# One group for the 64-column matmuls of a window pair in a shifted-window attention layer

## The reference

```python
# x: (16, 56, 56, 384) f32; 12 heads of 32; windows of 7x7 = 49 tokens; image shifted by 3
x + attention(group_norm(x, 32 groups))
# attention(x):
x = roll(x, (-3, -3)); q, k, v = split(x @ w_qkv.T)              # per window and head
dots = q @ k.T * 32 ** -0.5 + pos_emb[relative] + mask           # 49 x 49
out = softmax(dots) @ v
out = roll(out @ w_out.T + b_out, (3, 3))
```

## Time and profile before

| | |
|---|---|
| median of 3 runs | 4584.31 us |
| profiled execution | 4584.81 us, of which its span is 4583.0 us |
| mean granted TensorE clock | 0.998 |
| busy share | PE 96%, PEld 65%, DVE 88%, ACT 50%, POOL 50% |
| the chain that ended last | PE 74%, DVE 16%, issue 7%, ACT 2% |

### The profile page before, as it was taken

One profiled execution on the slowest core, in us unless ns is written; L12 is line 12 of the kernel. 1 busy time (PEld: TensorE's weight loads), 2 busy tenths in 40 slices (PEclk: granted clock), 3 DMA queues, 4 the chain that ended last, 5 costly groups with the idle time before them and its releaser, 6 DMA issues.

```text
span 4583.0 us, 164167 instructions
## 1 busy us (share of the span) xinstructions
PE 4390.2 (96%) x64360; PEld 2981.1 (65%) x64360; DVE 4046.9 (88%) x9283; ACT 2275.8 (50%) x4225; POOL 2282.0 (50%) x1933
## 2 busy tenths in 40 slices
PE   3999999999999999999999999999999999999998
PEld 1666666666666666666666666666666666666665
DVE  5898898989989998898989989899898988999886
ACT  0555555455554545555555455555555555555554
POOL 1455445455554554555455455545545545554454
PEclk9999999999999999999999999999999999999999
DMA  4344344334343433443343443334434433434332
GB/s 122 103 106 107 99 107 116 94 108 114 99 109 105 108 104 103 107 109 98 105 119 95 108 112 100 107 106 108 105 97 109 115 95 107 115 98 108 98 95 60
DMA packets 231099, 478.93 MB, mean 105 GB/s; under 512 B 39009, under 2 KB 140898, under 8 KB 222818
## 3 DMA queue, kind: packets, MB, share of 16 engines
q1 hardware_dynamic: 230338, 468.43, 38.6%
HBM read 159.99 MB, written 77.07 MB: 52 GB/s over the span
## 4 chain that ended last, share of the span: by engine, by line
PE 74%; DVE 16%; issue 7%; ACT 2%; SPq 0%; DMA 0%; POOL 0%; DVEq 0%; POOLq 0%; ACTq 0%
PE ps_pj L1087 24%; PE ps_pj L1083 13%; PE ps_post L1181 13%; PE ps_post L1172 5%; PE ps_sa L1121 4%; PE ps_st L1121 3%; PE ps_pv L1165 2%; DVE mt L928 2%; PE ps_st L1150 2%; PE ps_pv L1164 2%; PE ps_pv L1163 2%; DVE atl L907 2%; DVE mw L917 2%; PE ps_pj L1071 2%; DVE st L701 1%
## 5 line engine op out<-in xcount | busy, mean ns | idle before, releaser
L554 POOL TENSOR_TENSOR pl<-pf,ph 64x588 f16<-64x588 f32 x512 | 732.1, 1430 | 1622.3 <-ACT ph L669 1595.0
L599 ACT ACTIVATE qk<-ps_pj 128x392 f16<-128x392 f32 x768 | 381.9, 497 | 978.7 <-PE ps_pj L1087 978.7
L669 ACT ACTIVATE ph<-ps_st,sc 64x588 f16<-64x588 f32 x1024 | 772.5, 754 | 6.5
L1087 PE MATMUL ps_pj<-xh,wh 128*128 128x392 f16 x2304 | 765.2, 332 | 5.5 <-POOL xl L529 4.6
L1087 PE MATMUL ps_pj<-xh,wl 128*128 128x392 f16 x2304 | 764.6, 332 | 0.0
L1087 PE MATMUL ps_pj<-xl,wh 128*128 128x392 f16 x2304 | 764.5, 332 | 0.0
L575 POOL TENSOR_TENSOR rb<-tq,cst 128x588 bf16<-128x588 bf16 x512 | 701.2, 1370 | 48.1 <-ACT tq L658 8.1
L529 POOL TENSOR_TENSOR xl<-xn,xh 128x392 f16<-128x392 f32 x384 | 343.4, 909 | 599.0 <-DVE vl L860 293.0
L865 DVE TENSOR_TENSOR qk<-ps_pj,qk 128x392 f16<-128x392 f32 x768 | 432.8, 564 | 228.3 <-ACT qk L599 225.4
L664 ACT ACTIVATE pf<-ps_st,sc 128x588 f32<-128x588 f32 x512 | 384.7, 751 | 359.1 <-PE ps_st L1121 359.1
L953 DVE TENSOR_TENSOR pl<-pf,ph 64x588 f16<-64x588 f32 x512 | 543.4, 1061 | 0.5 <-ACT ph L669 0.5
(11 more groups left out here) (107 smaller groups left out, 9582.0 us busy)
## 6 DMA issues: line engine op xcount, KB each, us to landing
stack<-qk SPq DMA_DIRECT2D x1536, 147.0 KB
sx<-in_x SPq DMA_DIRECT2D x66, 1176.0 KB, 7.0
xs<-in_x SPq DMA_DIRECT2D x384, 84.0 KB
out<-xb SPq DMA_DIRECT2D x384, 84.0 KB
xs<-in_x SPq DMA_DIRECT2D x384, 63.0 KB
out<-xb SPq DMA_DIRECT2D x384, 63.0 KB
xs<-in_x SPq DMA_DIRECT2D x128, 66.0 KB
out<-xb SPq DMA_DIRECT2D x128, 66.0 KB
```

Source lines behind the costliest of these rows:

```text
L554: nc.gpsimd.tensor_tensor(pl[PAD:, :, PAD:PAD + N], pf[PAD:, :, :], ph[PAD:, :, PAD:PAD + N], ALU.subtract).then_inc(s_pl[1], 1)
L669: e = nc.scalar.activation(ph[rows, :, w * PAD:w * PAD + N].rearrange("p (a h) n -> p a h n", a=2), ps_st[rows, :, 0:HH * N].rearrange("p ...
L1087: m = mm(ps_pj[bank][:, 0:RT].rearrange("p (w n) -> p w n", w=NW), wa[:, c, o:o + 128], xa[:, b, c, :, 0:N], **on)
```

## The change

`transposed_scores` writes its bias with four matmuls of 64 output partitions instead of two of 128, and all of a pair's bias matmuls come before its 24 score matmuls. On PE, `transposed_scores(t - 1)` moves to the start of step k, directly ahead of `scores(t)`, and `shift_rows(t)` moves up from behind `project_out` to directly behind `attend`. The other engines' orders are changed to match: ACT takes `pf` first and `tq` before `ph` and `xh`; DVE makes the maxima before `atl` and the first slot's units; POOL makes `rb(t)` before `pl(t - 1)`, and the residual last.

```diff
 # POOL, step()
                     if not (tk.last and k >= 4):
                         x_lows(tk, k)
-                    if not (tk.last and k + 3 >= 8):
-                        residual(t + 3, n, k + 3)
-                    if not (tk.first and k < 1):
-                        split_probabilities(t - 1, ...)
-                        pool.wait_ge(s_pl[1], t)
-
                     pool.wait_ge(s_tc, t + 1)
+                    need(pool, s_st, t)
                     nc.gpsimd.tensor_tensor(
                         rb[:, :, :, :], ...
                         ALU.mult).then_inc(s_rb, 1)
+                    if not (tk.first and k < 1):
+                        split_probabilities(t - 1, t + 1)
+                        pool.wait_ge(s_pl[1], t)
+                    if not (tk.last and k + 3 >= 8):
+                        residual(t + 3, n, k + 3)
 # ACT, step()
+                    if not (tk.first and k < 1):
+                        probabilities(t - 1)
                     if not (tk.first and k < 3):
                         attended_high(t - 3)
                     if not (tk.last and k >= 4):
                         units(tk, k, 0)
+                    shift_rows(t)
+                    if not (tk.first and k < 1):
+                        probabilities_high(t - 1)
+                    if not (tk.last and k >= 4):
                         x_highs(tk, k)
                         units(tk, k, 1)
-                    if not (tk.first and k < 1):
-                        probabilities(t - 1)
-                    shift_rows(t)
-                    if not (tk.last and k >= 4):
                         units(tk, k, 2)
 # DVE, step()
                     logits(t, tk, k)
                     maxima(t, k)
-                    if not (tk.last and k >= 4):
-                        units(tk, k, 0)
-                    if not (tk.first and k < 3):
-                        attended_low(t - 3)
...
                     maxima_low(t)
+                    if not (tk.first and k < 3):
+                        attended_low(t - 3)
+                    if not (tk.last and k >= 4):
+                        units(tk, k, 0)
 # PE, transposed_scores()
                 for hh in range(2):
-                    out = ps_st[:, hh, 0:HH * N]
-                    mm(out, bt[:, kind, :], rb[:, hh, :, :].rearrange("p h n -> p (h n)"),
-                       start=True, stop=False, skip_group_check=True)
+                    for w in range(2):
+                        rows = slice(w * PAD, (w + 1) * PAD)
+                        mm(ps_st[rows, hh, 0:HH * N], bt[:, kind, rows], rb[:, hh, :, :].rearrange("p h n -> p (h n)"),
+                           start=True, stop=False, skip_group_check=True)
+                for hh in range(2):
                     m = score_blocks(ps_st, odd, p, hh, True, start=False, stop=True, skip_group_check=True)
 # PE, step()
+                    if not (tk.first and k < 1):
+                        transposed_scores(t - 1, *back(tk, k, 1))
                     scores(t, tk, k)
...
                         attend(t - 2, *back(tk, k, 2))
+                    shift_rows(t)
                     if not (tk.last and k >= 4):
                         units(tk, k, 1)
-                    if not (tk.first and k < 1):
-                        transposed_scores(t - 1, *back(tk, k, 1))
                     if not (tk.first and k < 3):
                         project_out(t - 3)
-                    shift_rows(t)
```

More of the change, by code:

```diff
@@ L545, in _, with split_probabilities @@
                 residual(j, 0, j)
[L547 to L551, removed]
+            def split_probabilities(t, spread):
+                pool.wait_ge(s_rb, spread)
                 pool.wait_ge(s_ph, t + 1)
@@ L567, in step @@
                         x_lows(tk, k)
-                    if not (tk.last and k + 3 >= 8):
-                        residual(t + 3, n, k + 3)
-                    if not (tk.first and k < 1):
-                        split_probabilities(t - 1, n * 6 + 6 + sum(len(x_before(tk, i)) for i in range(min(k + 1, 4) if tk.last else k + 1)))
-                        pool.wait_ge(s_pl[1], t)
                     pool.wait_ge(s_tc, t + 1)
+                    need(pool, s_st, t)
                     nc.gpsimd.tensor_tensor(
@@ L585, in _ @@
                 image(m)
-            split_probabilities(8 * (LAST + 1) - 1, 6 * LAST + 6)
+            split_probabilities(8 * (LAST + 1) - 1, 8 * (LAST + 1))
         @block.scalar
@@ L665, in probabilities, with probabilities_high @@
                                      scale=sc[:, 0:1])
+            def probabilities_high(t):
                 need(act, s_pv, t)
@@ L681, in _ @@
             end = 8 * (LAST + 1)
+            probabilities(end - 1)
             attended_high(end - 3)
-            probabilities(end - 1)
+            probabilities_high(end - 1)
             attended_high(end - 2)
@@ L1217, in _ @@
             end = 8 * (LAST + 1)
+            transposed_scores(end - 1, Tick(B - 1, PARTS - 1), 7)
             transpose_attended(end - 3, 5)
             attend(end - 2, Tick(B - 1, PARTS - 1), 6)
-            transposed_scores(end - 1, Tick(B - 1, PARTS - 1), 7)
             project_out(end - 3)
```

## The result

The changed kernel takes 5712.41 us (median of 4 runs, 5708.64 to 5730.28), the kernel before 4583.78 us (median of 4): ratio 1.2469, 95% interval 1.2441 to 1.2496. The forecast was 5800 us in 5150 to 6050. The profiled execution has a span of 5707.6 us at a mean granted clock of 0.903, against 0.998 before.

A forecast was written before the change was run, and what follows sets the result against it. PE, busy 96%, was taken as the bound. Half ticks growing from 34.94 to 40.6 us add 720 us over 127, giving 5305; 495 us of clock falls make 5800 us, range 5150 to 6050.

The forecast's parts named there:

- The crossings: PE switches between 64-column and full-width matmuls: six a step become two, 0.09 us each, 190 us saved.
- The loads: Late fourth residual on POOL delays SP's row loads; PE stands 4.4 us before step 1's x unit, making that step 13.6.
- `rb`: In steps 2 and 3 POOL's `rb` comes late behind `xl`, delaying the next bias; steps become 9.6 and 8.8 us.
- the sum: All four steps of a half tick: 40.6 us against 34.94, 5.7 more, for 127 half ticks 720 us.
- The clock: PE's clock halves behind each of three stalls a half tick, 1.3 us each, 495 us in all.
- the long stall: PE's wait for the loaded row in step 1, put at 4.4 us, with 1.3 us of clock cost behind it.
- the short ones: PE's waits for `rb` at the ends of steps 2 and 3, put at 2.4 and 1.9 us, 1.3 us clock cost each.
- the step that let every stall longer than 1.0 us be followed by half clock: PE idled 1.0 us before a clock fall near the run's end, so all three longer stalls were charged 1.3 us.
- The sign of a PEclk row below 9 throughout: Expected on the changed kernel's profile page: granted-clock row below 9 throughout, from clock falls at the stalls.
- Only `rb` is late: Rival: loads on time, only steps 2 and 3 stall; 4750 us, or 5080 with two clock falls; chance 0.13.
- Clock only after the long stall: Rival: half clock follows only step 1's stall, 5520 us, or none at all, 5305; chance 0.25.
- Faster: Rival: saved crossings come back and nothing new is late; 190 us less, 4395 us; chance 0.05.

The follow-up runs named there:

- The one part alone: Kernel before, with only the bias written as four 64-wide matmuls ahead of all 24 transposed score matmuls, no order moved: 4544.87 us, ratio 0.9915.
- Residual first: Changed kernel with POOL's residual put first in each step again: 4969.21 us, ratio 1.0841.
- the residual moved alone: Kernel before with only POOL's residual moved behind `pl` and `rb`, and `pl`'s wait count lowered to match: 5829.95 us, ratio 1.2717.
- `xh` early: Changed kernel with ACT making `xh` ahead of the first slot's unit, `tq` and `ph`: 5165.35 us, ratio 1.1267.
- the filled stall: Changed kernel with 75 unused matmuls added on PE ahead of x0 in steps 1 and 5: 5447.39 us, ratio 1.1887.
- both edits: Changed kernel with POOL's residual first in each step and ACT's `xh` ahead of the first slot's unit: 4438.37 us, ratio 0.9683.

## Why the prediction was right

- **The crossings.** Right: 2523.63 to 2523.89 is 0.26, and one such start a step is left on the way in. The one part alone gave 0.2 us for two crossings in the steps where PE waits for nothing. The four bias matmuls take 0.28 us to the first score matmul (0.25 forecast), side by side. What the prediction called 64-column bias work is of no worth by itself.
- **The loads.** Right in every link: 9.65 us from the first issue to the start (9.8), 3.98 us of standing here and 3.7 on average (470.1 / 126; 4.4 forecast), a step 1 of 13.5 us where it had no half clock (13.6). Residual first took 743 us away, and the residual moved alone brought 1246.
- **`rb`.** Right: from `tq`'s start to `rb`'s 4.09 us in the step 2 shown (0.25 + 1.52 + 0.68 + 1.77 = 4.2 forecast), waits of 490 us over the run, and `xh` early took 547 us away. The steps' lengths were put at 9.6 and 8.8; measured 9.3 and 9.8, the second with the clock's part in it and 8.8 without. All four steps at full clock came to 40.1 us a half tick, where the sum had 40.6.
- **The clock.** Right for the long stall, half right for the short ones. The forecast took the same 1.3 us for each of three stalls, 495 us in all.
  - The long stall cost more: 2.1 us by the filled stall (265 us), and 16.2 less 13.5 = 2.7 us by step 1 with and without half clock, in 108 of 126 cases (some 290 us).
  - The short ones cost less, because the step that let every stall longer than 1.0 us be followed by half clock failed: 147 of the 252 stalls for `rb` were followed by none. Where half clock came, steps 3 and 0 were 1.5 us longer (10.3 against 8.8, 10.0 against 8.5), so 105 x 1.5 = some 160 us, 0.6 us a stall. No kernel of its own was run for this, and `xh` early gives no cleaner number: of its 547 us, PE's waits explain 490 less the 92 that came new for `mt` (126.4 against 34.1), about 400, and of the 150 left some 60 fall in step 1, which came down from 15.8 to 15.35.
  - Together 415 to 450 us, where 495 were forecast, and some 675 to 715 of the measured 1128 for the steps at full clock, where 720 were forecast. That the clock's sum came out near is partly luck: one price was too low and the other, taken twice, too high. The sign of a PEclk row below 9 throughout did not come either; the row alternates between 8 and 9.
  - What decides which short stall is followed by half clock stays open. Not its length: in the filled kernel the 108 that were lasted 1.95 us on average, the 144 that were not 1.97.
- **The rivals.** "Only `rb` is late" is out by the residual alone; the kernel that it describes is residual first, and its 4969 us lie in the 4750 to 5080 that this rival had. "Clock only after the long stall" is out by the window at 2549.30 and by residual first, which has no long stall and still a clock of 0.955, though it holds for more than half of the short stalls. "Faster" needed `xl` without the wait for `ph`, and loads in time as well: with both edits it came true, 146 us where the forecast's sum had 190.

## What to carry to other kernels

When an order is moved, follow each moved instruction to the DMA that waits for it, not only to the engine: a residual of 1.0 us that nobody on the cores was short of held back 7.8 us of DMA issues, and its slack was under 1 us (the x unit started 10.45 us behind the first issue before, and 9.65 where it waited). A chain of in-order engines that are each half idle can still bound the kernel, so count latencies from the wait that starts it to the one that ends it. And price a stall of TensorE twice, once for the standing and once for the clock that may fall behind it; then look at whether matmuls with nothing to compute would be cheaper.

## What was not expected of the hardware

- At half clock 1107 us of the changed kernel were run, of the filled one (1 - 0.965) x 2 x 5442.8 = 381 us: 726 us of half clock cost 265 us, 0.37 us each and not 0.5. A part of it falls on the standing itself: in the window 2529.20:2533.30 above, 4.1 us with PE busy 0.27, the granted clock is already 0.88.
- Longer stalls came with longer half clock, but much of it fell on the standing. With the residual alone late, PE stood for 8.15 us, and the run was at half clock for (1 - 0.882) x 2 x 5829.1 = 1376 us, 10.2 us of it at each of the 126 stalls; in the kernel with `xh` early, whose long stalls are of 3.7 us, it was (1 - 0.941) x 2 x 5161.1 = 609 us, 4.8 us for each of 126. Windows of the first, one stall (2538.2 to 2546.4) and the work behind it:

```profile
2538.30:2540.80 2.50, 0.00 (x0) 0.00 (x0) 0.85 (x2) 0.46 (x1) 0.00 (x0) 1.00 0.20 65
2540.90:2546.30 5.40, 0.00 (x0) 0.00 (x0) 0.00 (x0) 0.00 (x0) 0.00 (x0) 0.50 0.27 84
2546.40:2551.00 4.60, 4.60 (x38) 3.07 (x39) 2.01 (x10) 2.16 (x3) 0.00 (x0) 0.50 0.09 30
```

- DVE's `mt` cast of 24 columns took 0.18 us, or 0.81 where POOL's `xl` ran beside it. It was so in the kernel before too, in step 2 beside `xl` (0.83 on average) and in step 3 beside the residual (0.92). Up to 0.64 x 125 = 80 us of PE's waits for `mt` with both edits could come from it; no run here shows what they would be without it.
